# A fused attention and expert layer on one core: the router as ranks in 14 steps, and a new order of the steady batch

## The chip, the cores and the metric

The kernel runs on one core of a Trainium2 chip. The metric is the device time of one execution in microseconds (us); less is better.

## What is computed

The input x is 4 batches of 1024 rows of 128 channels. With `ln` for a layer norm without weights:

```
x = x + ln(attn(ln(x)));   attn(y) = y + ripple(y)
x = x + ln(ffn(ln(x)))
ripple: q, k, v = y @ Wqkv, 8 heads of 16
        every row looks at the rows 0, 1, 2, 4, ... 512 above it (11 terms), softmax over them
        + a causal convolution of v with 7 taps for each channel
        + linear attention (elu(q)+1, elu(k)+1) over the whole batch;  then @ Wo
ffn:    scores = sigmoid(y @ gate_W) * route_scale; the best 2 of 8 experts, their scores
        divided by their sum; sum over them of gate * (gelu(y @ W1[e] + b1) @ W2[e] + b2)
        + gelu(y @ Ws1 + bs1) @ Ws2 + bs2
```

## The kernel before, in words

Five engines run programs written out by hand: PE (matmuls, and transposes as matmuls with an identity), DVE, ACT, POOL and SP (which issues loads, stores and copies). Semaphores connect them; each engine takes its instructions in the written order. So the order of the calls in each engine's loop `for b in range(B + 1)` is the schedule, and nothing else plans it.

A batch is handled in two layers that overlap. In the round b the engines do the attention of batch b, and beside it the expert layer of the two halves of batch b-1: the units u0 = 2b-2 and u1 = 2b-1 of 512 rows each. The fifth round (b = 4) has only the expert layer of the last batch. Rounds 1 and 2 are the steady ones; round 3 has no next batch to prepare.

The steps of a round, by the names of the code:

- DVE: `residual(2b-2)` closes the first half of the former batch and opens the round. Then the key and query features (`key_features`, `query_features`), three groups of `products` (q times a shifted k, L284), `stats` of the batch after (L904), `linear_state` (its `kv` is L961), `residual(u1)`, the router `gates(u0)` (L1105 to L1155), `softmax_logits`, `gate_hidden(u0)` (L1164), `softmax_weights`, and eight tiles of `weigh` (L1021), which make the 11 weighted terms of each row, with the steps of `gates(u1)` among them. `add_conv` (L1041) adds the convolution to a finished half.
- PE: `sum_heads` (L1366) sums the products, `turn_scores`, `low`, `gates_expert_major` turns the gates, `hidden` (L1460) and `experts_out` (L1500, a tile of 128 rows with five matmuls) are the expert layer; `turn_x3`, `gate_logits` and `turn_logits` begin a unit; `sum_terms` (L1395, L1398) adds the terms of a tile; `turn_x`, `project_k`, `project_q`, `project_v` make the next batch's keys, queries and values. `keep_busy` (L1509) turns the identity, with no result that anything reads.
- ACT: copies PSUM to SBUF (L573), scales the convolution's taps (`scale_taps`, L640), normalises (`normalise1`, L584, for the next batch; `normalise3`, L698, for a unit of the expert layer), takes the squares of the norms (`norm2`, `norm3_squares`, `norm4`), and all of Exp and Gelu. Exp and Gelu are in different tables, and each change of table is an ACT_TABLE_LOAD.
- POOL: `ln1` to `ln4` raise variances to the power -1/2, and `sum_taps_first`, `_second` and `_third` issue copies between tiles in SBUF that add one scaled tap to another.
- SP: loads of x, 19 copies per batch that shift v by 1 to 64 rows (`shift_v`), stores.

The router of a unit (`gates`) works on a tile of 128x32 (four tiles of rows, 8 experts). Before the change it has 24 steps, one DVE instruction each, that wait for one another: sigmoid (0 to 2), the largest score and the first expert that has it (3 to 7), the same for the second (8 to 13), weights (14 to 18), and the gates as a sum of three bf16 parts (19 to 23). Steps 0 to 3 of u0 stand between the third products and `kv`; the others behind `residual(u1)`. The 24 steps of u1 are spread over the tiles 1 to 4 of `weigh`, six for each.

A few waits matter below. `scores` on ACT needs `sum_heads(b, 2)`, which needs `kv`. The tile j of `weigh` needs `sum_terms(j-4)`. `add_conv(b, 0)` needs `sum_terms(3)` and the sum of all taps. `residual(2b)` needs `ln2`, that needs `norm2(2b)`, that needs `output(b, 0)`; on ACT, `norm2(2b)` stands behind `key_parts` and `query_parts` of the next batch.

## Time and profile before

| | us |
|---|---|
| three runs | 281.3, 281.8, 281.28 |
| median | 281.3 |
| the profiled execution | 281.24 |
| its span, first to last instruction | 279.5 |
| PE busy | 252.3 (90%) |
| DVE busy | 234.2 (84%) |
| ACT busy | 188.7 (68%) |
| POOL busy | 88.0 (31%) |

The span is the time between the first and the last instruction of the profiled execution; 1.74 us of its time lie around it. PE is busy with `keep_busy` too, so its share says less than it seems. The chain of waits that ended last is made of PE by 56%, ACT by 20%, DVE by 14%, POOL by 4%. The granted TensorE clock is 0.99 of full speed in the mean.

### The profile page before, as it was taken

Reading aid. Unit: us, or ns where it says so; the run is one execution under the profiler, and the core shown is the slowest. Engines: PE = TensorE matmul, PEld = TensorE weight load, DVE = VectorE, ACT = ScalarE, POOL = GpSimd, SP = SyncE. Lnnn points to the kernel's source line nnn. Section 1 sums busy time; section 2 is a strip of 40 time slices with the busy share of each in tenths; the row PEclk is TensorE's granted clock in tenths of the full one; section 3 lists DMA queues with packets and bytes.
Section 4 is the critical chain, followed back from the end, with each engine's and each line's share of the span. In section 5 each row is a group of like instructions: output and inputs, shape, how many; then the busy total and the mean of one; then the engine's idle time right before and its main releaser. Section 6 shows DMA issues by size and latency. Waiting matters only on the chain.

```text
span 279.5 us, 4820 instructions
## 1 busy us (share of the span) xinstructions
PE 252.3 (90%) x1640; PEld 175.4 (63%) x1640; DVE 234.2 (84%) x615; ACT 188.7 (68%) x444; POOL 88.0 (31%) x144
## 2 busy tenths in 40 slices
PE   5899999895988899998978899998989799999993
PEld 5444656885435686787635686787646677884483
DVE  7799899879988867999889967999599899858933
ACT  2482256638978766949798767959798546557831
POOL 5960300045471124044562114044232132431013
PEclk9999999997999999999999999999999999999998
DMA  7437801000799954401799972101799963000012
GB/s 194 100 98 242 236 19 59 1 0 5 218 230 196 233 113 83 121 1 38 245 234 208 211 137 43 49 5 32 244 217 228 230 122 73 17 0 1 0 40 75
DMA packets 23395, 32.12 MB, mean 115 GB/s; under 512 B 3958, under 2 KB 17103, under 8 KB 23371
## 3 DMA queue, kind: packets, MB, share of 16 engines
q1 hardware_dynamic: 20346, 21.59, 27.0%
q0 software_dynamic: 3024, 10.22, 20.1%
q8 instruction: 13, 0.21, 0.3%
q14 instruction: 12, 0.09, 0.1%
HBM read 5.07 MB, written 2.10 MB: 26 GB/s over the span
## 4 chain that ended last, share of the span: by engine, by line
PE 56%; ACT 20%; DVE 14%; POOL 4%; issue 3%; DMA 1%; POOLq 0%; DVEq 0%; ACTq 0%
PE psH L1398 11%; PE psF L1460 7%; PE psY L1500 6%; PE psG L1320 4%; PE psA L1366 4%; PE psA L1292 4%; DVE prods L284 3%; PE psA L1500 3%; POOL rstd L468 2%; ACT squares L691 2%; ACT xn L584 2%; ACT xn L698 2%; PE psG L1486 2%; DVE prods L1021 2%; PE psH L1395 2%
## 5 line engine op out<-in xcount | busy, mean ns | idle before, releaser
L284 DVE TENSOR_TENSOR prods<-qT,kT 128x1024 f32<-128x1024 f32 (+1 forms) x48 | 50.7, 1111 | 2.7 <-PE psA L1366 1.6
L466 POOL TENSOR_SCALAR var<-ss 128x4 f32<-128x4 f32 (+1 forms) x24 | 8.3, 345 | 102.0 <-ACT squares L684 46.3
L1398 PE MATMUL psH<-ident,prods 128*128 128x128 f32 x324 | 40.0, 273 | 0.0
L468 POOL TENSOR_TENSOR rstd<-var,neg_half 128x4 f32<-128x4 f32 (+2 forms) x27 | 38.1, 1412 | 2.2
L1398 PEld LDWEIGHTS psH<-ident,prods 128*128 128x128 f32 x324 | 36.4, 141 | 2.9 <-issue 2.9
L1021 DVE TENSOR_TENSOR prods<-v_shift,prob 128x896 f32<-128x896 f32 x32 | 34.6, 1082 | 0.0
L1460 PE MATMUL psF<-x3T,w 128*128 128x512 f32 x58 | 29.4, 614 | 1.4 <-ACT hid L722 1.4
L1366 PE MATMUL psA<-prods,slot_sel 128*32 128x512 f32 x168 | 23.0, 598 | 3.4 <-DVE kv L961 2.3
L722 ACT ACTIVATE hid<-psF,b1c 128x512 f32<-128x512 f32 x29 | 19.2, 690 | 6.6 <-PE psF L1460 6.5
L1164 DVE TENSOR_TENSOR hid<-hid,psG 128x512 f32<-128x512 f32 x30 | 19.3, 681 | 3.3 <-PE psG L1486 3.3
L1021 DVE TENSOR_TENSOR prods<-v_tok,prob 128x128 f32<-128x128 f32 (+2 forms) x60 | 20.8, 369 | 0.1
L1292 PE MATMUL psA<-xnT,wqkv 128*128 128x512 f32 x36 | 17.2, 601 | 1.5 <-ACT xnT L573 1.5
L1500 PEld LDWEIGHTS psY<-w,hid 128*128 128x128 f32 x140 | 16.6, 192 | 1.5 <-issue 1.4
L1500 PE MATMUL psY<-w,hid 128*128 128x128 f32 x140 | 17.6, 277 | 0.0
L1460 PEld LDWEIGHTS psF<-x3T,w 128*128 128x128 f32 x58 | 9.5, 189 | 11.1 <-issue 8.6
L1366 PEld LDWEIGHTS psA<-prods,slot_sel 128*32 128x32 f32 x168 | 5.4, 108 | 17.4 <-issue 8.3
L691 ACT ACTIVATE squares<-x,neg_mean 128x128 f32<-128x128 f32 x24 | 9.3, 391 | 8.7 <-DVE x L1052 8.7
L1320 PE MATMUL psG<-vT,tapT 128*128 128x512 f32 x28 | 12.8, 596 | 0.0
L1509 PE MATMUL psG<-ident 128*128 128x128 f32 x62 | 9.6, 321 | 3.1 <-POOL ident L419 3.1
L698 ACT ACTIVATE xn<-x,nmr,rstd 128x128 f32<-128x128 f32 x24 | 9.8, 482 | 3.7 <-POOL nmr L519 3.7
L1041 DVE TENSOR_TENSOR prods<-psH,convT 128x512 f32<-128x512 f32 x8 | 5.5, 692 | 8.1 <-PE psH L1398 7.9
L584 ACT ACTIVATE xn<-x_in,nmr,rstd 128x128 f32<-128x128 f32 x24 | 9.9, 487 | 3.2 <-POOL nmr L484 3.2
(247 smaller groups left out, 590.9 us busy)
## 6 DMA issues: line engine op xcount, KB each, us to landing
v_shift<-v_tok SPq DMA_DIRECT2D x20, 448.0 KB
convT<-tapT POOLq DMA_DIRECT2D x6, 512.0 KB, 6.0
x_res<-L_attn_x SPq DMA_DIRECT2D x4, 512.0 KB, 9.5
out<-y_out SPq DMA_DIRECT2D x7, 256.0 KB, 2.3
x_in<-L_attn_x SPq DMA_DIRECT2D x3, 512.0 KB, 4.0
v_shift<-v_tok SPq DMA_DIRECT2D x4, 384.0 KB
tapT<-tapT POOLq DMA_DIRECT2D x3, 512.0 KB, 11.5
convT<-kexp POOLq DMA_DIRECT2D x3, 512.0 KB, 9.1
```

What stands on the lines that cost most here:

```text
L284: return eng.tensor_tensor(prods[:, QUADS * (s % 2) + q, t0:t1], qT[:, t0:t1], kT[:, PRE - off + t0:PRE - off + t1], ALU.mult)
L468: return nc.gpsimd.tensor_tensor(rstd[:, cols], var[:, cols], neg_half[:, cols], ALU.pow)
L584: nc.scalar.activation(xn[:, j, :], x_in[:, j, :], ACT.Identity, bias=nmr1[:, j:j + 1], scale=rstd1[:, j:j + 1]).then_inc(xn_ready, 1)
L722: nc.scalar.activation(hid[:, c, half_cols(u)], hidden_bank(u, c), ACT.Gelu, bias=b1c[:, c:c + 1]).then_inc(hidden_free, 1)
L1021: return nc.vector.tensor_tensor(dst, src.rearrange("p m (h d) -> p m h d", d=HD), w, ALU.mult)
L1164: nc.vector.tensor_tensor(hid[:, c, cols], hid[:, c, cols], spread_bank(u, c), ALU.mult).then_inc(gated, 1)
L1292: pe.matmul(psA[:, half, :], wqkv[:, bass.ts(part, P)], xnT[(b + 1) % 2][:, bass.ts(half, HALF)], start=True, stop=True).then_inc(psA_full, 1)
L1320: ins = pe.matmul(psG[:, half, :], tap_diag[:, TAPS - 1 - tap, :], vT[:, VPRE - tap + half * HALF:VPRE - tap + (half + 1) * HALF], start=( ...
L1366: ins = pe.matmul(psA[32 * q:32 * q + 32, half, :], ksum_sel[:] if low else slot_sel[:, s, :], fqT[:, cols] if low else prods[:, QUADS * ( ...
L1398: ins = pe.matmul(dst, terms[:, j % TERM_BUFS, m, :], ident[:], is_transpose=True, start=False, stop=(m == live[-1]))
L1460: pe.matmul(hidden_bank(u, c), w1[:, bass.ts(c, P)], x3T[:, half_cols(u)], start=True, stop=True).then_inc(hidden_full, 1)
L1500: ins = pe.matmul(output_tile(u, n), hid[:, c, bass.ts(j, P)], w2[:, c, :], start=(c == CH - 1), stop=(c == CH - 2))
```

## The change

It has five parts.

1. **Router.** `gates` has 14 steps. Steps 3 to 5 compare each score with each other one of its row (128x256 elements, in the tile `above`, which lies in `folded`), with a constant `tie_bar` that lets the lower expert win a tie, and count how many are above it. A rank under 1.5 is one of the best two. The tail takes four steps instead of five. The steps of u0 all stand behind `residual(u1)`; those of u1 stand in the tiles 2 to 4 of `weigh`, 4 + 6 + 4.
2. **ACT in a round.** `normalise1` of the next batch goes from around `scores` to behind the exponentials, among `normalise3(u1)`, `evacuate_x3` and `evacuate_shared`; `norm3_squares(u1)` goes behind `scores`; `evacuate_q` goes behind `scale_outputs(u0)`, the last step before `key_parts`; the values and keys by rows (`token_major_v`, `token_major_fk`) go ahead of the first tap; `norm4` of the former u1 goes behind the taps 2 and 3.
3. **PE in a round.** `turn_x` goes from ahead of the exponentials to behind `turn_logits(u1)`, `project_k` among the terms at j = 1 and `project_q` at j = 5, `output(b, 0)` from j = 4 to j = 6. The 18 turns of `keep_busy` become 8 and 8; the 14 ahead of `output(b, 1)` become a tile of `experts_out(u1)`.
4. **POOL in a round.** `ln1(b+1)` goes from ahead of the first tap sum to behind `ln3(u1)`, ahead of the second.
5. **The last rounds.** In round 3 two tiles of `experts_out(u1)` stand around the last `sum_terms`; the first unit of the last batch is normalised by DVE, the second by ACT (before: the other way about); in round 4 `keep_busy` goes, `experts_out(u0-1)` is split around `gate_logits`, and `gate_hidden` follows the steps 6, 9, 14 and 14 of `gates(u1)`.

The diff, cut to its core:

```diff
@@ gates @@
-                    elif n == 3:
-                        ins = red(m1, score, AX_X, ALU.max)
-                    elif n == 4:
-                        ins = tt(eq, score, spread(m1), ALU.is_equal)
...
+                    elif n == 3:
+                        ins = tt(above, score.unsqueeze(2).to_broadcast(pair), score.unsqueeze(3).to_broadcast(pair),
+                                 ALU.subtract)
+                    elif n == 4:
+                        ins = tt(above, above, tie_bar[:].unsqueeze(1).to_broadcast(pair), ALU.is_gt)
+                    elif n == 5:
+                        ins = red(rank, above, AX_X, ALU.add)
+                    elif n == 6:
+                        ins = nc.vector.scalar_tensor_tensor(out=both, in0=rank, scalar=1.5, in1=score,
+                                                             op0=ALU.is_lt, op1=ALU.mult)
...
@@ DVE, round @@
-                    products(b, 2, range(0, 1))
-                    products(b, 2, range(1, 3), gate_step_of(u0, 0))
-                    linear_state(b, gate_step_of(u0, 2))
+                    products(b, 2)
+                    linear_state(b)
...
-                        gates(u0, range(4, 24))
+                        gates(u0, range(N_GATE_STEPS))
...
@@ POOL, round @@
-                    if more:
-                        ln1(b + 1)
                     if b >= 2:
                         ln4(u0 - 1)
-                    if b:
+                    if b == 0:
+                        ln1(b + 1)
+                    else:
                         sum_taps_first(b)
                         ln3(u1)
+                        if more:
+                            ln1(b + 1)
                         sum_taps_second(b)
...
@@ PE, round @@
-                        if more and j == 1:
+                        if more and ffn and j == 1:
+                            project_k(b + 1)
+                        if more and j == (5 if ffn else 1):
                             project_q(b + 1)
                         sum_terms(b, j)
-                        if j == TPH:
+                        if j == (6 if ffn else TPH):
                             output(b, 0)
+                        if not more and j >= 6:
+                            experts_out(u1, (j - 6,))
...
@@ the round's last lines on DVE @@
                     else:
-                        gate_hidden(u1, range(2, 4))
+                        last_normalise()
```

**ACT, third round, around the exponentials** (L672, L680 after: the exponentials; L584, L592: `normalise1`; L691, L699: `norm3_squares`; `prods<-psA`: `scores`). Before:

```order
L584 ACTIVATE xn<-x_in,nmr,rstd 128x128 x4
L691 ACTIVATE squares,ss<-x,neg_mean 128x128 x4
L573 ACTIVATE prods<-psA 128x512 x2
L584 ACTIVATE xn<-x_in,nmr,rstd 128x128 x4
L722 ACT_TABLE_LOAD
L722 ACTIVATE hid<-psF,b1c 128x512 x2
L573 ACTIVATE gT<-psG 24x512
L573 ACTIVATE hid<-gT 24x512
L722 ACTIVATE hid<-psF,b1c 128x512 x2
L726 ACTIVATE hid<-gate_shared,bs1c 64x512
L672 ACT_TABLE_LOAD
L672 ACTIVATE prob<-prob 128x768
```

After the change:

```order
L581 ACTIVATE prods<-psA 128x512 x2
L699 ACTIVATE squares,ss<-x,neg_mean 128x128 x4
L730 ACT_TABLE_LOAD
L730 ACTIVATE hid<-psF,b1c 128x512 x2
L581 ACTIVATE gT<-psG 24x512
L730 ACTIVATE hid<-psF,b1c 128x512 x2
L581 ACTIVATE hid<-gT 24x512
L734 ACTIVATE hid<-gate_shared,bs1c 64x512
L680 ACT_TABLE_LOAD
L680 ACTIVATE prob<-prob 128x768
L706 ACTIVATE xn<-x,nmr,rstd 128x128 x4
L592 ACTIVATE xn<-x_in,nmr,rstd 128x128 x4
```

Both halves of `normalise1` have left the stretch from the scores to the exponentials and stand behind them.

**ACT, third round, its end** (L722, L730: Gelu of `hidden`; squares of psY: `norm4(u0)`; L755, L763: `scale_outputs`; L647, L655: the first part of `key_parts`). Before:

```order
L722 ACT_TABLE_LOAD
L722 ACTIVATE hid<-psF,b1c 128x512 x2
L746 ACTIVATE squares,ss<-psY 128x128 x4
L573 ACTIVATE qT<-psA 128x512 x2
L755 ACTIVATE y_out<-psY,rstd 128x128 x4
L722 ACTIVATE hid<-psF,b1c 128x512 x2
L726 ACTIVATE hid<-gate_shared,bs1c 64x512
L573 ACTIVATE gT<-psG 24x512
L573 ACTIVATE hid<-gT 24x512
L647 ACT_TABLE_LOAD
L647 ACTIVATE kexp<-kT 128x1024
```

After:

```order
L730 ACT_TABLE_LOAD
L730 ACTIVATE hid<-psF,b1c 128x512 x2
L581 ACTIVATE kT<-psA 128x512 x2
L730 ACTIVATE hid<-psF,b1c 128x512 x2
L754 ACTIVATE squares,ss<-psY 128x128 x4
L734 ACTIVATE hid<-gate_shared,bs1c 64x512
L581 ACTIVATE gT<-psG 24x512
L581 ACTIVATE hid<-gT 24x512
L763 ACTIVATE y_out<-psY,rstd 128x128 x4
L581 ACTIVATE qT<-psA 128x512 x2
L655 ACT_TABLE_LOAD
L655 ACTIVATE kexp<-kT 128x1024
```

The copies of the queries (`qT`) stood ahead of `scale_outputs` and two Gelu; now they are the last work before the table load.

**PE, third round, among the terms** (L1500, L1478: `experts_out`; L1460, L1438: `hidden`; L1292, L1270: a projection; L1395 with L1398, L1373 with L1376: `sum_terms`). Before:

```order
L1292 MATMUL psA<-xnT,wqkv 128x512 x2
L1395 MATMUL psH<-ident,prods 128x128
L1398 MATMUL psH<-ident,prods 128x128 x9
L1460 MATMUL psF<-x3T,w 128x512 x2
L1395 MATMUL psH<-ident,prods 128x128
L1398 MATMUL psH<-ident,prods 128x128 x10
L1395 MATMUL psH<-ident,prods 128x128
L1398 MATMUL psH<-ident,prods 128x128 x10
L1470 MATMUL psG<-identb,gparts 24x128 x4
L1395 MATMUL psH<-ident,prods 128x128
L1398 MATMUL psH<-ident,prods 128x128 x11
L1408 MATMUL psY<-wo,prods 128x128
```

After:

```order
L1478 MATMUL psY<-w,hid 128x128 x5
L1373 MATMUL psH<-ident,prods 128x128
L1376 MATMUL psH<-ident,prods 128x128 x10
L1438 MATMUL psF<-x3T,w 128x512 x2
L1373 MATMUL psH<-ident,prods 128x128
L1376 MATMUL psH<-ident,prods 128x128 x10
L1448 MATMUL psG<-identb,gparts 24x128 x4
L1373 MATMUL psH<-ident,prods 128x128
L1376 MATMUL psH<-ident,prods 128x128 x11
L1464 MATMUL psG<-gT,gate_sel 128x512 x2
L1270 MATMUL psA<-xnT,wqkv 128x512 x2
L1373 MATMUL psH<-ident,prods 128x128
```

The first rows are the projection (queries) before, and after it the last tile of `experts_out(u0)`; the queries now follow the fifth tile of terms.

## Rows read from the trace of the kernel before

**Rows 1.** Busy time by stage: stretch, length, PE, PEld, DVE, ACT, POOL, clock, DMA
```profile
59.23:121.24 62.01, 55.24 (x362) 38.08 (x360) 53.75 (x139) 49.56 (x110) 21.50 (x23) 0.97 0.59 135
121.24:184.22 62.98, 58.45 (x402) 41.34 (x400) 54.65 (x144) 50.45 (x118) 21.90 (x25) 1.00 0.55 129
184.22:247.11 62.89, 57.70 (x416) 42.57 (x414) 54.58 (x140) 45.23 (x121) 20.63 (x26) 1.00 0.56 130
247.11:279.50 32.39, 27.20 (x162) 18.34 (x162) 19.92 (x79) 16.29 (x45) 5.19 (x9) 0.96 0.08 25
```

**Rows 2.** Waits of DVE: us in total, times, longest us
```profile
DVE gtmp L1105 <- ACT gexp L714: 9.4, 6, 2.4
```

**Rows 3.** Timeline, DVE, third batch: start us, us, line, operation
```profile
140.46 0.28 DVE L961 TENSOR_TENSOR kv<-psY,head_mask 128x128 f32<-128x128 f32 x1
143.81 0.18 DVE L1113 TENSOR_TENSOR gtmp<-gtmp,gmax 128x32 f32<-128x32 f32 x1
148.02 0.18 DVE L1155 CAST gparts<-gtmp 128x32 bf16<-128x32 f32 x1
```

**Rows 4.** Groups by shape, DVE: count, busy us, mean ns, idle before
```profile
L967 DVE TENSOR_TENSOR folded<-prob 128x384 f32<-128x384 f32 x8 | 4.4, 555 | 0.8 <-ACT prob L672 0.6
L1021 DVE TENSOR_TENSOR prods<-v_tok,prob 128x256 f32<-128x256 f32 x8 | 3.3, 417 | 0.0
L919 DVE TENSOR_REDUCE row_mean<-w 128x5 f32<-128x640 f32 x1 | 0.8, 812 | 0.0
```

**Rows 5.** Timeline, PE, third batch
```profile
140.89 0.63 PE L1366 MATMUL psA<-prods,slot_sel 128*32 128x512 f32 x3 [0.89 <-DVE kv L961]
145.38 1.14 PE L1284 MATMUL psA<-ident,prods 128*128 128x128 f32 x8 [0.65 <-ACT prods L573]
152.01 1.04 PE L1284 MATMUL psA<-ident,xn 128*128 128x128 f32 x8
158.44 0.63 PE L1430 MATMUL psF<-ident,xn 128*128 128x128 f32 x4
174.49 0.39 PE L1470 MATMUL psG<-identb,gparts 128*24 128x128 bf16 x4
175.44 0.30 PE L1395 MATMUL psH<-ident,prods 128*128 128x128 f32 x1 [0.55 <-DVE prods L1041]
```

**Rows 6.** Timeline, ACT, third batch, middle
```profile
152.21 0.69 ACT L722 ACTIVATE hid<-psF,b1c 128x512 f32<-128x512 f32 x1 [0.59 <-PE psF L1460]
156.66 1.64 ACT L698 ACTIVATE xn<-x,nmr,rstd 128x128 f32<-128x128 f32 x4
```

**Rows 7.** Timeline, ACT, POOL and DVE, end of the third batch
```profile
176.19 1.28 ACT L647 ACT_TABLE_LOAD   x1
177.48 1.06 ACT L647 ACTIVATE kexp<-kT 128x1024 f32<-128x1024 f32 x1
182.78 1.03 POOL L468 TENSOR_TENSOR rstd<-var,neg_half 128x4 f32<-128x4 f32 x1
184.22 1.11 DVE L1052 SCALAR_TENSOR_TENSOR x<-psY,rstd,x_res 128x128 f32<-128x128 f32 x4
```

**Rows 8.** Timeline of PE after two gaps, and the busy times at the first
```profile
66.03 1.97 PE L1284 MATMUL psA<-ident,vT 128*128 128x128 f32 x8 [2.87 <-ACT vT L573]
218.89 0.63 PE L1430 MATMUL psF<-ident,xn 128*128 128x128 f32 x4 [1.84 <-ACT xn L698]
66.00:67.00 1.00, 0.96 (x5) 0.97 (x6) 1.00 (x2) 0.97 (x2) 0.90 (x1) 0.50 0.00 0
```

**Rows 9.** Timeline, POOL, second and fourth batch
```profile
75.80 2.57 POOL L468 TENSOR_TENSOR rstd<-var,neg_half 128x8 f32<-128x8 f32 x1
227.09 0.86 POOL L487 DMA_DIRECT2D convT<-tapT  x1 [7.21 <-DMA convT<-fkT]
```

**Rows 10.** Timeline, DVE, last part
```profile
251.44 0.18 DVE L1105 TENSOR_SCALAR gtmp<-gexp 128x32 f32<-128x32 f32 x1 [1.49 <-ACT gexp L714]
256.75 0.18 DVE L1155 CAST gparts<-gtmp 128x32 bf16<-128x32 f32 x1
```

265 lines of the change are left out of this document (115 added, 150 removed).

## The prediction

> **What bounds the kernel now.** I read the busy times by stage first. I cut the span where DVE starts `residual(2b)`, since the whole round hangs on it, and the last part where PE starts the front of the last batch [rows 1]. The rounds 1, 2 and 3 take 62.01, 62.98 and 62.89 us, the last part 32.39. In round 2 PE is busy for 58.45, DVE for 54.65, ACT for 50.45: all three are dense, none is the bound alone. So the shares don't price an edit; the chain through a round does. The waits say where DVE, which does the router, stands still: 9.4 us in six waits for the exponentials of the router's logits [rows 2]. I then followed round 2 through the timelines and give its times from its start (121.24 us = 0).
>
> In round 2 the chain is this. DVE starts `kv` at 19.2 [rows 3]; PE sums the scores from 19.65, and turns them from 24.1, held by ACT, whose `norm3_squares` and first half of `normalise1` stand ahead of the copy of the scores [rows 5]. The last Gelu of u0 starts at 31.0, `normalise3(u1)` at 35.4 [rows 6], `turn_x3(u1)` on PE at 37.2, the turn of the gates behind the fourth tile of terms at 53.25 [rows 5]. From there DVE has its last four tiles, and ACT ends with a table load at 54.95 and the key and query parts; POOL's `ln2` lets DVE start the next round at 62.98 [rows 7].
>
> **The router.** A chained step on 128x32 costs DVE 0.22 us: 19 of them from 143.81 to 148.02 [rows 3]. Steps 0 to 2 stay. Steps 3 and 4 are now 128x256: 0.42 us is the row for that many elements, 0.56 that for 384 [rows 4]; I take 0.45 with the chain's gap. For the reduction of 256 elements the row has 640 in 0.81 us [rows 4]; 0.42 lies between that over 2.5 (0.33) and 0.5. For u0: 0.86 (steps 0 to 2), 0.45 + 0.45 + 0.42, and eight steps of 0.22, is 3.9 us, where 0.75 + 4.4 stood before: 1.2 less. For u1 the hidden gaps make it 1.0 less. Of these 2.2 us per round only what lies ahead of the scores can reach the chain, below. With both bounds of the new steps (3.7 and 4.5 us) u0's gates end at 23.8 to 24.6, and PE wants them at 24.5, so this price hardly matters in the steady rounds.
>
> **The front of a round.** Steps 0 to 3 of u0 (0.75 us) and their wait (one of the six of [rows 2], about 1 us) leave the stretch ahead of `kv`: it starts at 17.6, not 19.2. PE starts the last sums of scores at 18.0. ACT has only the copies of the scores to do, and PE's 0.65 us of waiting for them [rows 5] goes. Its queue (sums 1.86, two `hidden` 1.75, the turn 0.97, `low` 1.9, from differences of starts) ends at 24.5. Then the turn of the gates, two `hidden`: the last Gelu of u0 starts at 26.7, 4.3 us sooner. From that Gelu to `normalise3(u1)` ACT took 4.45 us [rows 6]; without the copies of `turn_x` (0.96) and with the gates' row (0.6) it takes 4.1: 30.8. PE follows 1.78 later, at 32.5 instead of 37.2. What hides the moved `normalise1`: in the old place it was in this chain, 3 us of ACT; in the new one half of it delays the x3 copy by 0.3.
>
> **The middle.** From `turn_x3(u1)` to the turn of u1's gates PE took 16.05 us, without a gap worth naming [rows 5]. The same work now has `turn_x` in it, 0.97 (152.01 to 152.98 [rows 5]); `project_k` stands where `project_q` stood. With 0.4 us of waits for ACT's two copies this is 17.3: 49.8, 3.4 us sooner. DVE is at 45.4 by then and waits.
>
> **The end of a round.** Here the time goes again. `add_conv(b, 0)` and the restart of the terms take 0.95 us (174.49 to 175.44 [rows 5]), the tile 1.3, two spreads 0.5, `project_q` 1.7: PE has the queries at 54.3. ACT has been full since 48.7 (last Gelu, `norm4`, shared Gelu, gates, `scale_outputs`, which waits for POOL). It ends the copy of the queries at 55.1. From the table load to DVE's start of the next round it took 8.03 us [rows 7], of which DVE was late by 0.3, since `ln2` ended at 183.81 [rows 7]: 7.7. The round is 62.8 us long. So round 1 gets 0.8 us longer and round 2 0.2 shorter: DVE's and PE's head start of 4 us ends in a wait for `norm2(2b)`, which stands behind the key and query parts. Their table load starts at 55.1, no sooner than the 54.95 of before [rows 7], since the work between `turn_x3(u1)` and it has grown from 17.8 to 22.6 us.
>
> What else is moved: the 18 + 14 turns of `keep_busy` cost nothing as work, and neither does their going. `ln1(b+1)` on POOL took some 5 us in round 1, its power alone 2.57 [rows 9], and now stands ahead of the second tap sum. That starts at 28.7 instead of 28.6, for the first one starts 2.3 us sooner; the queue of four sums ends at 47 or 48 and is wanted at 49.9. SP's 19 copies of v start 2.1 us sooner, because `token_major_v` is ahead of the first tap; their terms are wanted 2.7 sooner, with some 5 us to spare in round 2. The load of the next x waits for `normalise1`, 10 us later than before, but stands in SP's queue behind a store that is later still. All of these at nothing.
>
> **Round 3 and the last part.** Without `stats` the front gains another 0.9 us: `turn_x3(u1)` at 31.3. PE has no projection in the middle: the fourth tile is done at 45.7. But the sum of taps ends there: its last addition was issued at 42.9 after 7.2 us of waiting [rows 9], and the terms that follow may wait half a us for it. Behind it `output(b, 0)` now comes after the seventh tile, at 54 instead of 51.3, then `norm2`, `ln2`, `residual`, `last_normalise`: I get 0.6 us less than the 62.89 [rows 1]. In the last part the gates of u0 took 5.4 us [rows 10], now 4.0; but PE's queue and ACT's four Gelu wait for the second table load, 0.8 us later. Walked through, the last experts end 0.5 us sooner.
>
> **TensorE's clock.** PE stood idle for 2.87 us at the start of round 1, and behind that the clock is 0.50 of full, its 1.2 GHz level; eight turns took 1.97 us, where 1.14 is usual [rows 5, 8]. Behind a gap of 1.84 us in round 3 it was full [rows 8]. In the new order PE ends its last `keep_busy` ahead of `turn_x3(u1)` at 29.5 in round 1, 30.2 in round 2 and 29.3 in round 3, so the gaps are 3.0, 2.3 and 2.0 us. I take a fall in round 1 alone. The old fall cost 1.2 us of PE's work; here a part lies under waits for ACT: 0.8. The bounds are 0 and 1.3 for each of three rounds. The Trainium skill, "TensorE: Matmul & The Clock Gate", Part 4: PE-mode transpose, says that a transpose doesn't count as PE busy. By that rule `keep_busy`, which is nothing but transposes, would hold no clock, and the clock would fall in all three rounds. The trace speaks against it: 24 transposes and the gap of 1.84 us left the clock full.
>
> **The sum.** Round 1 +0.8, round 2 -0.2, round 3 -0.6, last part -0.5, clock +0.8: +0.3 us on the profiled execution's 281.24, which is 0.06 below the median. I forecast 281.5 us: no change that 0.2% (0.56 us, about what a measurement of this kernel can tell) would show.
>
> The Trainium skill, "ScalarE: Activation LUTs", What ACT_TABLE_LOAD costs, has 2.66 us for a change of table. In the trace it is 1.29, from 176.19 to 177.48 [rows 7], and I use that. By the page's figure the two changes on the new chain would make the round an estimated 65.5 us.
>
> **Rivals.**
> - *The order fits better than I walk it* (faster). The small waits that I put in (0.4 for the copies, 0.95 at `add_conv`, 0.5 at the taps) go under one another, and the clock stays up. For it: PE ran its 16.05 us without such waits [rows 5], and an error in the middle counts in three rounds. Against it: each wait has a row like it. Without the fall, and with 1 us less in each round, it is 281.24 - 0.5 - 3.1, about 277.6 us. Chance 0.3.
> - *The clock falls in all three rounds* (slower). The point is a gap between 1.84 and 2.87 us; the gaps of 2.3 and 2.0 lie between. Three falls at 1.2 us each on the 280.7 without one give 284.3; it decides in `turn_x3(u1)`, which the chain passes. Against it: the fall behind 2.87 us began only after 2 us of idling, and the two shorter gaps end about there. Chance 0.25.
> - *The change doesn't do what it says*: the ranks give the same gates with 10 instructions fewer, and the orders above show that the moves are made. I give this no chance.
>
> Chances: forecast 0.45 (of which 0.12 under 280.7 and 0.13 over 281.9), fast rival 0.3, slow rival 0.25. Faster by over 0.2% is 0.12 + 0.28 = 0.40, same 0.22, slower 0.13 + 0.25 = 0.38. The range reaches from near the fast rival to near the slow one: 277.8 to 284.2. The forecast's own case is 280.3 to 282.7.
>
> **What would show it.** Right: `turn_x3(u1)` 32 to 33 us behind the start of rounds 1 and 2, the turn of u1's gates at 49 to 50.5, ACT without a gap from the last Gelu to `norm2(2b)`, DVE waiting about 1.5 us for POOL ahead of `residual(2b)`, rounds of 62.3 to 63.3. The first gates of a unit take 3.7 to 4.5 us. A granted clock of 0.5 in round 1 around 32 us. Wrong: rounds under 61.5 us with ACT waiting at their end, or a wait of `add_conv` for a DMA, or 0.5 behind `turn_x3(u1)` in all rounds.

## The result, and the profile after

The changed kernel takes 290.25 us in the median of four runs (288.8 to 290.31), before takes 281.34 (281.28 to 281.8). The ratio is 1.030, with a 95% interval of 1.028 to 1.032: slower by 8.9 us. I had forecast 281.5 us and a range up to 284.2. The ratios in this document leave disturbed executions out, as the comparisons do.

| | before | after |
|---|---|---|
| profiled execution | 281.24 us | 290.23 us |
| its span | 279.5 us | 288.4 us |
| PE busy | 252.3 us (90%) | 252.3 us (87%) |
| DVE busy | 234.2 us (84%) | 227.8 us (79%) |
| ACT busy | 188.7 us (68%) | 189.2 us (66%) |
| mean granted clock | 0.990 | 0.966 |

The stages first, cut as in [rows 1]: rounds 1, 2 and 3 and the last part (stretch, length, then the busy time of PE, its weight loads, DVE, ACT and POOL, the granted clock, DMA).

```profile
59.15:125.35 66.20, 58.74 (x375) 39.86 (x373) 52.15 (x119) 49.87 (x110) 19.58 (x23) 0.95 0.55 127
125.35:190.55 65.20, 58.11 (x385) 40.72 (x384) 53.18 (x123) 50.86 (x118) 22.43 (x25) 0.97 0.54 125
190.55:255.50 64.95, 56.06 (x377) 40.54 (x377) 53.26 (x117) 43.63 (x117) 19.57 (x26) 0.95 0.54 125
255.50:288.40 32.90, 26.43 (x152) 17.48 (x152) 17.82 (x64) 17.61 (x50) 6.38 (x11) 0.96 0.08 25
```

Against [rows 1] that is +4.19, +2.22, +2.06 and +0.51 us. The time doesn't come from more work: in all, DVE is busy for 6.4 us less, PE for as long as before, ACT for 0.5 us more. What changed with the length of the rounds is the clock: 0.95, 0.97, 0.95, where it was 0.97, 1.00 and 1.00.

Where does it fall? PE's timeline at the last sums of scores in round 1, and at `turn_x3(u1)` and the turn of the logits behind it in all three rounds:

```profile
77.19 0.73 PE L1344 MATMUL psA<-prods,slot_sel 128*32 128x512 f32 x3 [3.12 <-DVE kv L968]
...
79.34 1.14 PE L1344 MATMUL psA<-prods,slot_sel 128*32 128x512 f32 x3
...
93.39 0.63 PE L1408 MATMUL psF<-ident,xn 128*128 128x128 f32 x4 [2.70 <-ACT xn L706]
...
98.85 0.41 PE L1420 MATMUL psF<-ident,gate_shared 8*128 8x8 f32 x4
...
143.40 0.63 PE L1344 MATMUL psA<-prods,slot_sel 128*32 128x512 f32 x3 [0.96 <-DVE kv L968]
...
158.69 0.63 PE L1408 MATMUL psF<-ident,xn 128*128 128x128 f32 x4 [2.05 <-ACT xn L706]
...
164.00 0.41 PE L1420 MATMUL psF<-ident,gate_shared 8*128 8x8 f32 x4
...
222.07 1.09 PE L1408 MATMUL psF<-ident,xn 128*128 128x128 f32 x4 [2.04 <-ACT xn L706]
...
228.47 0.41 PE L1420 MATMUL psF<-ident,gate_shared 8*128 8x8 f32 x4
```

And the granted clock, over one us at the last sums of round 1 and behind each of the three `turn_x3(u1)` (stretch, length, PE busy, clock, DMA):

```profile
78.00:79.00 1.00, 1.00 (x8) 0.50 0.93 242
95.00:96.00 1.00, 1.00 (x4) 0.50 0.89 180
160.00:161.00 1.00, 1.00 (x7) 0.50 1.04 206
222.00:223.00 1.00, 0.93 (x5) 0.50 0.89 194
```

At 0.50 PE runs on its 1.2 GHz level, at 1.00 on 2.4. Read the fence ahead of it by durations: a sum of three at 77.19 takes 0.73 us, one at 79.34 takes 1.14, the usual (143.40) is 0.63. The last sums of round 1 take 3.23 us (77.19 to 80.42), where those of round 2 take 1.85. From `turn_x3(u1)` to the end of the turn of the logits (start to start of the work behind it) it is 5.80, 5.65 and 6.75 us, and 3.99 us in round 2 of before (158.44 [rows 5] to 162.43). With the clock held it is 4.50, 4.51 and 3.99 in the new order, as the first experiment shows; in rounds 1 and 2 PE waits 0.28 us of it for ACT's copy of x3. So PE lost 1.4 us at the sums, and 1.3, 1.15 and 2.75 behind `turn_x3`. In that order the clock stays low for 3.4, 3.4, 3.4 and 6.8 us. I had forecast one fall, in round 1, for 0.8. The old fall at the start of round 1, behind the gap of 2.87 us [rows 8], is gone: PE turns the values at 63.08 without a wait.

Now the steps that I had named, in round 2 (125.35 us = 0), in the timelines: `kv`, the wait of `finish`, and the router's first step on DVE, the two turns of the gates on PE, and at the end ACT's table load, POOL's `ln2` and DVE's next round:

```profile
142.96 0.29 DVE L968 TENSOR_TENSOR kv<-psY,head_mask 128x128 f32<-128x128 f32 x1
144.09 1.13 DVE L1159 SCALAR_TENSOR_TENSOR y_out<-psG,rstd,x 128x128 f32<-128x128 f32 x4 [0.84 <-POOL rstd L471]
...
146.40 0.17 DVE L1108 TENSOR_SCALAR gtmp<-gexp 128x32 f32<-128x32 f32 x1
...
150.57 0.38 PE L1448 MATMUL psG<-identb,gparts 128*24 128x128 bf16 x4 [0.68 <-DVE gparts L1140]
...
177.23 0.39 PE L1448 MATMUL psG<-identb,gparts 128*24 128x128 bf16 x4
...
182.82 1.28 ACT L655 ACT_TABLE_LOAD   x1
...
189.42 1.03 POOL L471 TENSOR_TENSOR rstd<-var,neg_half 128x4 f32<-128x4 f32 x1
...
190.55 1.12 DVE L1058 SCALAR_TENSOR_TENSOR x<-psY,rstd,x_res 128x128 f32<-128x128 f32 x4 [1.75 <-POOL rstd L471]
```

`kv` starts at 17.6, as forecast. The gates' turn comes at 25.2 (forecast 24.5), `turn_x3(u1)` at 33.3 (32.5), the turn of u1's gates at 51.9 (49.8), the table load at 57.5 (55.1), the next round at 65.2 (62.8). The router is as forecast too: u0's first step at 146.40, its last ends at 150.43, 4.0 us (forecast 3.9).

### The profile page after: what moved, and what is told of

Read it like the earlier page. It is cut to its first block, busy times and chain, and to the rows that moved or that the text cites. A ratio compares the mean times of both kernels' runs of the same rounds, so it can differ in the third digit from the quotient of the medians.

```text
span 288.4 us, 4645 instructions
## 1 busy us (share of the span) xinstructions
PE 252.3 (87%) x1590; PEld 173.1 (60%) x1590; DVE 227.8 (79%) x535; ACT 189.2 (66%) x445; POOL 86.9 (30%) x139
## 4 chain that ended last, share of the span: by engine, by line
PE 57%; ACT 19%; DVE 13%; POOL 6%; issue 3%; POOLq 0%; DVEq 0%; ACTq 0%
PE psF L1438 9%; PE psH L1376 7%; PE psY L1478 7%; PE psA L1344 6%; POOL rstd L471 4%; PE psG L1298 4%; DVE prods L286 4%; PE psF L1415 3%; PE psA L1262 3%; ACT xn L706 3%; PE psA L1270 2%; PE psA L1478 2%; ACT squares L699 2%; POOL var L469 2%; PE psF L1408 1%
## 5 line engine op out<-in xcount | busy, mean ns | idle before, releaser
L469 POOL TENSOR_SCALAR var<-ss 128x4 f32<-128x4 f32 (+1 forms) x24 | 11.3, 471 | 127.9 <-ACT squares L754 66.8
L1376 PE MATMUL psH<-ident,prods 128*128 128x128 f32 x324 | 40.2, 273 | 0.0
L1376 PEld LDWEIGHTS psH<-ident,prods 128*128 128x128 f32 x324 | 36.4, 141 | 3.4 <-issue 3.4
L471 POOL TENSOR_TENSOR rstd<-var,neg_half 128x4 f32<-128x4 f32 (+2 forms) x27 | 37.0, 1370 | 2.2
L730 ACT ACTIVATE hid<-psF,b1c 128x512 f32<-128x512 f32 x29 | 19.4, 683 | 15.5 <-PE psF L1438 15.1
L1438 PE MATMUL psF<-x3T,w 128*128 128x512 f32 x58 | 28.7, 613 | 0.3 <-ACT gexp L722 0.3
L1344 PE MATMUL psA<-prods,slot_sel 128*32 128x512 f32 x168 | 24.2, 624 | 4.1 <-DVE kv L968 4.1
L1478 PEld LDWEIGHTS psY<-w,hid 128*128 128x128 f32 x140 | 20.2, 222 | 3.1 <-issue 3.1
L1478 PE MATMUL psY<-w,hid 128*128 128x128 f32 x140 | 21.0, 306 | 0.0
L1270 PE MATMUL psA<-xnT,wqkv 128*128 128x512 f32 x36 | 17.2, 601 | 0.3 <-ACT xnT L581 0.3
L1438 PEld LDWEIGHTS psF<-x3T,w 128*128 128x128 f32 x58 | 10.0, 194 | 11.1 <-issue 10.3
L699 ACT ACTIVATE squares<-x,neg_mean 128x128 f32<-128x128 f32 x24 | 9.3, 395 | 7.6 <-DVE x L1058 7.6
L1408 PE MATMUL psF<-ident,xn 128*128 128x128 f32 x28 | 4.9, 302 | 10.6 <-ACT xn L706 9.0
L1373 PE MATMUL psH<-ident,prods 128*128 128x128 f32 x32 | 9.1, 283 | 3.4 <-DVE prods L1047 2.5
L490 POOL DMA_DIRECT2D convT<-tapT x6 | 5.5, 919 | 20.6 <-DMA convT<-fkT 14.5
```

The source lines that it names most:

```text
L469: nc.gpsimd.tensor_scalar(var[:, cols], src, scale, EPS, ALU.mult, ALU.add).then_inc(step, 1)
L471: return nc.gpsimd.tensor_tensor(rstd[:, cols], var[:, cols], neg_half[:, cols], ALU.pow)
L730: nc.scalar.activation(hid[:, c, half_cols(u)], hidden_bank(u, c), ACT.Gelu, bias=b1c[:, c:c + 1]).then_inc(hidden_free, 1)
L1270: pe.matmul(psA[:, half, :], wqkv[:, bass.ts(part, P)], xnT[(b + 1) % 2][:, bass.ts(half, HALF)], start=True, stop=True).then_inc(psA_full, 1)
L1344: ins = pe.matmul(psA[32 * q:32 * q + 32, half, :], ksum_sel[:] if low else slot_sel[:, s, :], fqT[:, cols] if low else prods[:, QUADS * ( ...
L1376: ins = pe.matmul(dst, terms[:, j % TERM_BUFS, m, :], ident[:], is_transpose=True, start=False, stop=(m == live[-1]))
```

## The experiments

The theories: **the clock** (gaps on PE, which the new order makes and its fewer `keep_busy` turns don't fill, bring the clock down in each round, and PE is in the chain there), and against it **the new chain** (without any fall the new order is longer by itself, above all at the end of a round). A third: the router, or the sum of the taps, is what holds.

### More turns ahead of `turn_x3(u1)`

```diff
-FILL_LOW, FILL_LAST, FILL_K, FILL_OUT = 8, 8, 8, 14
+FILL_LOW, FILL_LAST, FILL_K, FILL_OUT = 8, 24, 24, 14
```

> The changed kernel with 24 turns instead of 8 in the last fill ahead of turn_x3(u1), in rounds 1 to 3. From turn_x3(u1) to the end of the turn of the logits PE took 5.80, 5.65 and 6.75 us in the three rounds of the changed kernel, where the same work took 4.06 in round 2 of before. Theory 1 (most of the loss is the clock, and idling of PE ahead of turn_x3(u1) brings it down): the gaps of 2.70, 2.05 and 2.04 us shrink to about 0.9, 0.3 and 0.3, the clock stays at its upper level behind them, the three stretches take 4.1 us each, and 6.0 us go: 284.2 us, bounds 283.2 and 285.5. Theory 2 (the new chain is longer by itself, and the clock is beside the chain): under 2 us go, 288.3 or more. Theory 3 (turns do not count as work for the clock, whatever their number): the clock falls as before and the time stays at 290.2.

Measured: 285.54 us in the median of four (284.57 to 288.49), ratio to before 1.014 (1.008 to 1.021). The work added makes the kernel 4.7 us faster. PE in round 1, at the last sums and at `turn_x3(u1)`, and at the start of round 2, where the clock still fell:

```profile
77.44 0.63 PE L1344 MATMUL psA<-prods,slot_sel 128*32 128x512 f32 x3 [3.12 <-DVE kv L968]
...
92.00 0.63 PE L1408 MATMUL psF<-ident,xn 128*128 128x128 f32 x4 [0.96 <-ACT xn L706]
...
96.16 0.41 PE L1420 MATMUL psF<-ident,gate_shared 8*128 8x8 f32 x4
...
126.25 1.52 PE L1262 MATMUL psA<-ident,vT 128*128 128x128 f32 x8 [1.86 <-ACT vT L581]
```

The median lies at the upper bound (285.5) that I had set for theory 1. The stretch from `turn_x3(u1)` (92.00) to the next work (96.50) is 4.50 us, in rounds 2 and 3 it is 4.51 (156.00 to 160.51) and 3.99 (219.16 to 223.15), and the clock is full behind all three gaps. What the kernel got instead are falls in another place, at `token_major_v` at the start of rounds 2 and 3: eight turns in 1.52 us behind a gap of 1.86. The changed kernel has a gap of 1.85 us in the same place, at 128.94, with the clock at 1.00 behind it. At the last sums the gap is 3.12 us, to the hundredth that of the changed kernel (77.19 above), and the clock stays up: a sum takes 0.63 us. Theory 1 holds, at 4.7 us and not 6.0. A part of the difference is that I had reckoned with 4.06 us for each of the three stretches, and two take 4.5. Another is round 3: its stretch is 2.75 us shorter than in the changed kernel, the round only 1.23 (63.72 us), and DVE waits 2.00 us for the tap sum at `add_conv(b, 0)` now. The new falls cost little where they are: round 2 of this execution is 64.05 us long with one, and 64.06 in the kernel with both fills below without one. Its round 1 is 63.26 us, 2.94 shorter than in the changed kernel, and 1.4 of that is the fall at the sums, which the edit didn't touch. Theory 3 of the list, that turns don't count, falls.

### Products instead of turns

```diff
-                    pe.transpose(bank[:, bass.ts(k % TPH, P)], ident[:], ident[:])
+                    pe.matmul(bank[:, bass.ts(k % TPH, P)], ident[:], ident[:], start=True, stop=True)
```

> The changed kernel with all fills as plain products of the identity with itself instead of transposes of it, the same number in the same places, so that all gaps stay as long as they are. Theory 1a (the length of the gap alone decides): the clock falls in the same places, 290.2 us. Theory 1b (transposes do not count for the clock, as the Trainium skill, TensorE: Matmul & The Clock Gate, Part 4: PE-mode transpose, has it, and products do): behind the gaps of 2.05 and 2.04 us in rounds 2 and 3 the clock stays up, and 4.3 us go: 286.0 us; behind the 2.70 us of round 1 it may fall still.

Measured: 286.69 us (285.75 to 290.5, four runs), ratio 1.015 (1.011 to 1.020). It tells less than I wanted: a product of fp32 runs as two instructions and takes twice as long as a turn, so the gaps of 2.05 us shrank to 0.79, and the gap, not the kind of work, may be what changed. The profiled run is the one of 290.5 us, with a start 3 us longer and a fall in the last part. But its three rounds are all at a full clock, so they show what the new order costs by itself (the kernel with both fills, below, has the same lengths in an execution of 285.99 us):

```profile
62.67:125.92 63.25, 59.04 (x405) 41.97 (x404) 51.98 (x120) 49.64 (x110) 19.03 (x23) 1.00 0.57 133
125.92:189.92 64.00, 58.36 (x401) 41.62 (x400) 53.08 (x123) 50.75 (x118) 22.39 (x25) 1.00 0.55 127
189.92:253.11 63.19, 54.99 (x393) 40.27 (x393) 53.30 (x117) 43.48 (x117) 18.24 (x26) 1.00 0.56 129
```

63.25, 64.00 and 63.19 us against 62.01, 62.98 and 62.89 [rows 1]: +1.2, +1.0, +0.3. To part kind and length I ran this, with fewer products:

```diff
-FILL_LOW, FILL_LAST, FILL_K, FILL_OUT = 8, 8, 8, 14
+FILL_LOW, FILL_LAST, FILL_K, FILL_OUT = 3, 3, 3, 14
...
-                        keep_busy(FILL_LOW, front(u1, X3))
+                        products_instead(FILL_LOW, front(u1, X3))
```

> The changed kernel, its two fills of 8 transposes of the identity ahead of turn_x3(u1) replaced by 3 products of it with itself each (a product of fp32 took two instructions and 0.27 us in the kernel with all fills as products, so 6 take about 1.6 us, where the 16 turns take 1.8), so that the gaps ahead of turn_x3(u1) are 2.2 us or longer in all rounds, no shorter than in the changed kernel. If the length of the gap decides: falls as in the changed kernel, mean clock 0.966, 290 us. If a transpose does not count as work for the clock and a product does: the clock stays up in rounds 2 and 3 at least, mean clock 0.98 or more, 286 us.

Measured: 288.68 us (288.25 to 290.57), ratio 1.027 (1.020 to 1.035), mean clock 0.97. The clock falls in all three rounds. The last fill and `turn_x3(u1)` in round 3:

```profile
217.30 0.94 PE L1486 MATMUL psF<-ident 128*128 128x128 f32 x6
220.43 1.09 PE L1408 MATMUL psF<-ident,xn 128*128 128x128 f32 x4 [2.20 <-ACT xn L706]
```

The clock over one us in round 2:

```profile
154.00:155.00 1.00, 1.00 (x6) 0.50 0.94 203
```

Products, and a gap of 2.2 us, and the turns of `turn_x3` still take 1.09 us instead of 0.63. The gap isn't the same everywhere: in round 1 it is 2.87 us, in round 2 only 1.75, and there the fall comes 1.1 us ahead of the gap, while PE is fully busy. The Trainium skill, "TensorE: Matmul & The Clock Gate", Part 4: PE-mode transpose, says that a transpose doesn't count as PE busy the way other work does. Neither run bears that out for the fp32 turns of this kernel: 24 turns in the last fill held the clock at `turn_x3(u1)`, and 3 products in place of each 8 turns, about as long, didn't. Per round, fills of 3.9 us of turns and of 4.1 us of products (all fills as products) held it; 2.2 us of turns and 1.9 us of products didn't.

### No fill at all

```diff
-FILL_LOW, FILL_LAST, FILL_K, FILL_OUT = 8, 8, 8, 14
+FILL_LOW, FILL_LAST, FILL_K, FILL_OUT = 0, 0, 0, 14
```

> The changed kernel without the two fills of 8 turns ahead of turn_x3(u1), rounds 1 to 3: the gaps grow by 1.8 us to 4.5, 3.9 and 3.8 us. If turns count as work, the clock falls 1.8 us sooner and the granted clock is low over more of the gap and less or as much of the work behind it: 289 to 291 us. If turns do not count at all, nothing changes in any row behind the gap: from turn_x3(u1) to the end of the turn of the logits 5.8, 5.65 and 6.75 us as before, 290.2 us.

Measured: 290.01 us (289.01 to 290.18), ratio 1.029 (1.023 to 1.035), mean clock 0.964. The fall starts sooner. In round 2 it begins at 155.5, behind a wait of 1.33 us for the spread gates and 0.4 us ahead of the gap of 2.95 (the clock over one us in the gap, and where the fall ends):

```profile
156.00:157.00 1.00, 0.00 (x0) 0.50 1.11 313
162.00:163.00 1.00, 1.00 (x4) 0.81 0.49 98
```

The clock is low for 6.8 us from 155.5 on, in the changed kernel for 3.4 us from 159.5 on; the sooner and longer fall lies for a good part in the gap, and the round is as long (65.22 us against 65.20). So 16 turns of fill bought nothing (290.0 against 290.25), and 32 bought 4.7 us. A fill that is too short was no better than none here.

### A fill ahead of the last sums as well

```diff
+                    if b == 1:
+                        pe.wait_ge(front_free, upto(u0, N_FRONT, 2))
+                        keep_busy(FILL_SUMS, hidden_bank(u0, 0))
                     sum_heads(b, 2)
```

with `FILL_SUMS = 24`, on top of the 24 turns ahead of `turn_x3(u1)`.

> As the kernel with 24 turns ahead of turn_x3(u1), and 24 turns more ahead of the last sums of scores in round 1, where PE idles for 3.12 us until kv is there, and the sums then took 3.23 us instead of the 1.86 of round 2. Theory 1: the clock stays up there too, and 1.6 us more go than with the fill at turn_x3(u1) alone: 282.6 us. Theory 2: nothing more than that kernel.

Measured: 284.18 us in ten runs (283.49 to 285.99), ratio 1.009 (1.006 to 1.012). By stage:

```profile
60.86:124.11 63.25, 60.03 (x415) 42.79 (x413) 51.98 (x119) 49.76 (x110) 19.51 (x23) 1.00 0.58 133
124.11:188.17 64.06, 58.43 (x401) 41.41 (x400) 53.13 (x123) 50.76 (x118) 22.43 (x25) 1.00 0.54 127
188.17:251.37 63.20, 56.52 (x393) 41.63 (x393) 53.27 (x117) 43.73 (x117) 18.48 (x26) 0.97 0.56 129
251.37:284.30 32.93, 26.43 (x152) 17.49 (x152) 17.84 (x64) 17.62 (x50) 6.38 (x11) 0.96 0.08 25
```

Rounds 1 and 2 are clean, 63.25 and 64.06 us. Against the changed kernel that is -2.95, -1.14 and -1.75: the fills give back 5.8 of the 8.9 us, and 6.1 by the medians. The further gain on the fill at `turn_x3(u1)` alone is 1.4 us by the medians, but it can't be put on the sums: in the profiled run of that kernel the clock had not fallen there, with the gap of 3 us in place. It hadn't in the profiled runs with few products and with no fill either, with gaps of 3.13 us. The fall at the sums is in one profile, that of the changed kernel.

Round 3 has a fall at its start here too, from 193.1 to 196.5, and is as long as the clean one above (63.20 and 63.19): a fall there costs nothing.

### The router alone, in the old order

```diff
-N_GATE_STEPS = 24
+N_GATE_STEPS = 14
...
-                        gates(u0, range(4, 24))
+                        gates(u0, range(4, N_GATE_STEPS))
```

and the body of `gates` as changed.

> The kernel before with the router of 14 steps alone, in the old order (four steps beside the products, ten behind residual(u1); u1's in pairs among the terms). Theory A (in the old order the router is beside the chain, which goes through ACT's norm, copies and Gelu): 281.3 us, within 0.3. Theory B (DVE is in the chain between residual(u1) and the exponentials): 1.0 us less DVE time in each of rounds 1 to 3 and 1.3 in the last part: 277.5 to 280.

Measured: 282.55 us in ten runs (281.04 to 284.17), beside 281.48 for before in 19 runs (281.19 to 282.95); ratio 1.002 (0.999 to 1.004). The medians are 1.1 us apart, more than the 0.3 that I had allowed theory A, but the executions of both kernels spread over more than that, and theory B's 277.5 to 280 is ruled out. Its `normalise3(u1)` starts on ACT at 156.83, where before has 156.66 [rows 6]: the DVE time saved doesn't reach the chain through ACT. Theory A fits.

### The first expert tile ahead of `turn_x3(u1)`

```diff
+                        experts_out(u0, (0,))
                         turn_x3(u1)
-                        experts_out(u0, (0,))
-                        gate_logits(u1)
                         experts_out(u0, (1,))
+                        gate_logits(u1)
+                        experts_out(u0, (2,))
```

`FILL_LAST` and `FILL_K` are 14 here, the rest as in the kernel with both fills.

> The kernel with 24 turns ahead of turn_x3(u1) and 24 ahead of round 1's last sums (284.2 us), and now the first tile of u0's expert outputs, 1.12 us of PE, ahead of turn_x3(u1) in place of 10 of the turns; the other tiles move one place forward. Theory (behind turn_x3(u1) PE is the chain, in a stretch of 32 us without gaps): 1.1 us less in each of rounds 1 to 3, 280.9 us, provided DVE's last product with the spread gates is done by then. Rival (ACT, not PE, sets the end of the round): at most 0.3 us a round, 283.3 us.

Measured: 283.65 us in ten runs, from 280.98 to 288.25; ratio 1.003 (0.999 to 1.007). The best runs are the 280.9 that I had worked out, the median isn't. In the profiled run rounds 1 and 2 take 62.1 and 62.9 us, 1.1 less each than with both fills, as the theory has it. That run has 287.02 us, and in round 3 a low clock in dense work:

```profile
233.00:234.00 1.00, 1.00 (x5) 0.50 0.00 0
240.00:241.00 1.00, 1.00 (x7) 0.50 0.00 0
```

PE had waited 1.91 us for `add_conv(b, 0)` up to 231.47; from 232.3 to 242.5 it is busy without a gap, and the clock is 0.50 all the time, 10.2 us. The falls of the changed kernel last 3.4 or 6.8 us. I have no cause for one of 10.

### The queries earlier

```diff
                             if j == 2:
-                                experts_out(u0, (3,))
-                            if j == 3:
                                 hidden(u1, range(2, 4))
+                            if j == 3:
+                                experts_out(u0, (3,))
...
-                        if more and j == (5 if ffn else 1):
+                        if more and j == (4 if ffn else 1):
```

and on ACT `evacuate_q(b + 1)` ahead of `scale_outputs(u0)`, in the kernel with both fills.

> The kernel with 24 turns ahead of turn_x3(u1) and 24 ahead of round 1's last sums (284.2 us), with the end of the round changed: hidden(u1) chunks 2 and 3 one tile earlier (ACT idled 3.67 us for them), project_q ahead of the fifth tile of terms instead of the sixth (PE idled 0.55 us there for add_conv), and ACT's copy of the queries ahead of scale_outputs, which waited 0.82 us for POOL. Theory (the end of a round goes through project_q, the copy of the queries and ACT's key and query parts, and that is where the head start of the front was lost): 1.5 us less in each of rounds 1 and 2, 281.2 us. Rival (the end hangs on output(b, 0) behind the seventh tile, not on the queries): within 0.5 us of 284.2.

Measured: 280.89 us in ten runs (280.12 to 281.64), ratio to before 0.997 (0.994 to 1.000). In round 2 (121.18 us = 0), on PE the turn of u1's gates and the queries, on ACT their copy and the table load, and DVE's next round:

```profile
171.87 0.39 PE L1450 MATMUL psG<-identb,gparts 128*24 128x128 bf16 x4
172.19 1.98 PE L1272 MATMUL psA<-xnT,wqkv 128*128 128x512 f32 x4
...
173.84 1.05 ACT L582 ACTIVATE qT<-psA 128x512 f32<-128x512 f32 x2
...
175.90 1.28 ACT L656 ACT_TABLE_LOAD   x1
...
183.62 1.13 DVE L1060 SCALAR_TENSOR_TENSOR x<-psY,rstd,x_res 128x128 f32<-128x128 f32 x4 [0.78 <-POOL rstd L472]
```

From the turn of the gates to the next round it is 11.75 us, where the changed kernel has 13.3. The wait at `add_conv` lies under the queries now, and ACT has no gap in that stretch. The expected 1.5 us in each of rounds 1 and 2 are there: rounds of 61.7, 62.4 and 62.2 us against 63.25, 64.06 and 63.2. This edit on the changed kernel, with its fills of 8 and none ahead of the sums:

> The changed kernel with the earlier queries alone, and its fills as they were (8, 8, none ahead of the sums). If the clock's loss and the end of the round are separate terms: the falls stay, mean clock 0.966, and 3.3 us go from 290.2: 286.9 us. If an earlier round hides the slow stretches, or the falls take the gain back: further off than 1 us.

Measured: 285.49 us (284.88 to 287.05), ratio 1.013 (1.009 to 1.017), mean clock 0.979: 4.8 us less than the changed kernel, not 3.3. The two terms aren't separate. In the profiled run the rounds take 62.9, 62.45 and 63.5 us: round 2 is as short as with the held clock (62.44), since it has no fall any more, and the fall at the sums of round 1 is gone too, with its gap of 3.12 us in place. Against that, the last part takes 34.1 us, with a fall from 250.9 on. The same gap of 2.04 us is there ahead of `turn_x3(u1)` in rounds 2 and 3, and the clock falls only at the second (four turns in 0.63 us, and in 1.09; that fall begins at 216.8, 0.6 us ahead of the gap's end):

```profile
156.72 0.63 PE L1409 MATMUL psF<-ident,xn 128*128 128x128 f32 x4 [2.04 <-ACT xn L706]
...
217.40 1.09 PE L1409 MATMUL psF<-ident,xn 128*128 128x128 f32 x4 [2.04 <-ACT xn L706]
```

### Both orders together, and what held them

The two diffs above in one kernel, with `FILL_LAST` and `FILL_K` 14 and `FILL_SUMS` 24:

> The two orders together: the first expert tile ahead of turn_x3(u1) with 14 turns in the last fill, and the earlier queries at the end of a round, with 24 turns ahead of round 1's last sums. If PE's 1.1 us per round and ACT's 1.6 us at the end of rounds 1 and 2 add up: 3.0 us under the 280.9 of the kernel with the earlier queries alone, 278 us, faster than before (281.35). If both shorten the same chain: 280 to 281. The kernel with the expert tile first had runs from 281 to 288 us with clocks of 1.0 to 0.964, so its best runs are what to compare, and the clock may fall here as well.

Measured: 12 runs from 277.19 to 286.3 us, median 282.17; ratio 0.988 (0.985 to 0.991), which rests on the four that took 277.2 to 279.4 us. The profiled execution isn't one of them, it took 282.22 us. Its rounds 1 and 2 take 60.6 and 61.1 us, so the tile ahead of `turn_x3(u1)`, with 10 turns fewer, is worth 1.1 and 1.35 us a round beside the kernel with the earlier queries, and the gains add up. Its round 3 takes 65.3. DVE waits 3.17 us there for the last addition of the tap sum, and a fall of the clock follows, from 230.3 to 233.7. The wait isn't new: with the clock held in the old tile order it was 2.00, 2.31 and 1.55 us in round 3 (24 turns, products, both fills). In round 3 of its timeline, the first addition of the tap sum on POOL, and DVE at `add_conv(b, 0)`:

```profile
199.09 0.93 POOL L491 DMA_DIRECT2D convT<-tapT  x1
...
229.97 0.69 DVE L1049 TENSOR_TENSOR prods<-psH,convT 128x512 f32<-128x512 f32 x1 [3.17 <-DMA convT<-tapT]
```

The same kernel with the router of 24 steps:

```diff
-N_GATE_STEPS = 14
+N_GATE_STEPS = 24
...
-                            first = 2 * (3 * (j - 2) + n - 1)
+                            first = 4 * (3 * (j - 2) + n - 1)
```

and the body of `gates` as before, with u1's steps four by four.

> As the kernel with both orders, but with the router of 24 steps: u0's gates take 5.15 us instead of 4.0, u1's steps go four by four beside the terms instead of two by two. If the router of ranks is beside the chain in the new order as it is in the old: within 0.5 us of the kernel with both. If PE's wait for u0's gates (0.6 us in round 2 before their turn) shows that DVE is in the chain there: 1.1 us in each of rounds 1 to 3 and 1.2 in the last part, 3 to 4.5 us slower.

Measured: 284.29 us in ten runs (282.89 to 290.88), ratio 1.006 (1.003 to 1.008). In the new order the router is in the chain, in rounds 2 and 3: PE waits 2.33 and 1.53 us for u0's gates, where the kernel with the ranks waits 0.39 and not at all; in round 1 neither waits. PE's waits by line (us in total, times, longest), and the wait of round 2:

```profile
PE psG L1467 <- DVE gparts L1159: 4.2, 3, 2.3
...
146.99 0.38 PE L1467 MATMUL psG<-identb,gparts 128*24 128x128 bf16 x4 [2.33 <-DVE gparts L1159]
```

The waits say 3.5 us. The medians of all runs are 2.1 us apart, but eight of the twelve with the ranks are over 281 us. The medians of those that the ratios rest on are 278.4 and 284.3, 5.9 apart, and the best runs 5.7. The 2 us beyond the waits can be the clock: behind the wait of 2.33 us it is low for 10.2 us, from 148.1 on. No run parts the two.

Last, the first two additions of the tap sum ahead of `ln4(u0-1)`:

```diff
-                    if b >= 2:
-                        ln4(u0 - 1)
                     if b == 0:
                         ln1(b + 1)
                     else:
                         sum_taps_first(b)
+                        if b >= 2:
+                            ln4(u0 - 1)
```

> As the kernel with both orders; on POOL the first two additions of the tap sum are issued ahead of ln4(u0-1) in rounds 2 and 3, not behind it. In round 3 of the kernel with both orders they were issued at 199.09, 2.6 us after the taps were scaled (196.6), the last of the four sums came late and DVE stood 3.17 us ahead of add_conv(b, 0) for it. Theory (the sum of taps through the DMA engines is what the new order runs into next): the additions go out 2.3 us or more sooner, the wait shrinks to 1 us or less, and the median falls from 282.2 to 279, with the best runs near 277. Rival (the DMA engines, 0.9 and more busy all through that stretch, set the end of the sums, not their start): the wait stays at 3 us, 282.

Measured: 278.33 us in ten runs (278.07 to 281.89), before 281.71 in the same comparison (281.17 to 283.13, 15 runs); ratio 0.990 (0.987 to 0.993). The same two rows of its timeline:

```profile
196.12 0.93 POOL L491 DMA_DIRECT2D convT<-tapT  x1 [7.07 <-ACT tapT L649]
...
227.30 0.69 DVE L1049 TENSOR_TENSOR prods<-psH,convT 128x512 f32<-128x512 f32 x1 [0.34 <-PE psH L1378]
```

And the three rounds:

```profile
59.40:120.01 60.61, 58.23 (x397) 40.88 (x395) 51.97 (x119) 49.56 (x110) 18.17 (x23) 1.00 0.59 138
120.01:181.37 61.36, 57.51 (x391) 40.41 (x390) 53.07 (x122) 50.58 (x118) 20.19 (x25) 1.00 0.58 133
181.37:243.52 62.15, 55.19 (x392) 40.07 (x391) 53.16 (x117) 43.62 (x117) 18.57 (x26) 1.00 0.57 131
```

The additions go out at 14.75 us of the round instead of 16.8 (2.05 sooner, a little less than I expected), and the wait for the DMA is gone. But the round 3 of 65.3 us is from an execution of 282.22 us, and the 62.15 from one of 278.15. The four best executions of the kernel without this edit have a median of 278.4 us and a ratio of 0.988: this one is no faster than they are. What differs is how many take over 281 us: 1 of 10, and 8 of 12 without the edit. Two sets of runs on two chips make that likely and don't show it. The edit has a price too: `ln4` comes later, and PE waits 0.68 us for u0's gates in round 2 (0.39 without it) and 1.10 in round 3 (none):

```profile
205.85 0.38 PE L1450 MATMUL psG<-identb,gparts 128*24 128x128 bf16 x4 [1.10 <-DVE gparts L1142]
```

This version beats both kernels: 1.0% less than before, 4% less than the changed kernel.

## Why the prediction was wrong

The miss is 8.75 us (290.25 against 281.5). The runs divide it so: the changed kernel has rounds of 66.2, 65.2 and 64.95 us; with the clock held (from the two kernels with clean rounds) they are 63.25, 64.05 and 63.2; I had 62.8, 62.8 and 62.3. So 5.9 us are the clock, of which I had 0.8 in the sum; 2.6 are the chain of the rounds; and 1.0 is the last part (32.9, I had 31.9).

- **The clock, +5.1. This is the step that failed:** "I take a fall in round 1 alone", at 0.8 us. There were two in round 1 and one in each of the others. I had looked at the gap ahead of `turn_x3(u1)` and read its length right (3.0, 2.3, 2.0 forecast; 2.70, 2.05, 2.04 measured). But I put a threshold between 1.84 and 2.87 us of gap, out of two cases. There is none in these runs: with 2.04 us the clock fell and did not fall in one execution, behind 1.86 it fell, with 3.12 it fell in the changed kernel and stayed in others. Its sign, 0.5 behind `turn_x3(u1)` in all rounds, was among those that I had named for being wrong. The slow rival (falls in all three rounds, chance 0.25) was the right mechanism. Its 284.3 was 6 us too low: 2.3 because it had 3.6 us for the clock, not 5.9 (no fall at the sums, and 1.2 us for each), and 3.6 in the rounds and the last part, which it took over from the forecast.
- **The gap that I left out.** I moved `kv` and found the sums of scores to start at 18.0 (right, 18.0). I didn't ask what PE would do until then. The work ahead of them ended sooner, because `token_major_v` and `token_major_fk` no longer wait behind the taps, and left 3.12 us idle in round 1: PE turns the values at 63.08 (66.03 [rows 8] before), and the last sums start at 77.19 (77.75 before). It is the same kind of view as the one I made at `turn_x3(u1)`, and I made it in one place only.
- **The price of a fall.** 1.2 us was the price of one that ran under eight turns. At `turn_x3(u1)`, where PE has dense work behind it, it is 1.15 to 2.75, and I had put the bound at 1.3. The 2.75 is the fall that lasts 6.8 us. At the start of rounds 2 and 3 of the kernels with the fills a fall of 3.4 us cost nothing in two rounds and half a us at most in a third.
- **The front, +0.85 in round 2** (the turn of the gates 0.7 late, `turn_x3(u1)` 33.35 against 32.5). u0's gates were right in length. But DVE began them late: `finish(u0-1)` waited 0.84 us for `ln4`, whose squares I had not followed on ACT behind taps 2 and 3. "This price hardly matters in the steady rounds" was wrong: PE waits 0.68 us for the gates, and 2.33 with 24 steps in the order of the last experiments.
- **The middle.** From `turn_x3(u1)` to the turn of u1's gates I had 17.3 us. With the clock held it is 17.4 (157.46 to 174.85 in the kernel with both fills); with the fall 18.5.
- **The end, +0.3.** From the turn to the next round I had 13.0, measured 13.3. That the head start would be lost there, behind ACT's queue, was right. It took one step more to see that the loss could be undone by the order of three calls.
- **Round 3, +0.9, and the last part, +1.0.** Round 3 has the same late gates and output as the others, and with the clock held PE waits 0.7 to 1.5 us at `add_conv(b, 0)`, behind the tap sum, where I had put half a us. In the last part I saw "the last experts end 0.5 us sooner"; it is 32.9 us against 32.39. One tile of u0's experts is done ahead of the last spreads, where before has two, so more of PE's work is left when the gates arrive. That is a reading of the order; I did no run on it, and the cause of the last part's 1.0 us stays open.
- **The tap sums at nothing:** right for this kernel, partly by luck. At `add_conv(b, 0)` in its round 3 DVE waits 2.72 us for PE, whose clock was low in that round. With the clock held ahead of it DVE waits 1.5 to 2.3 us for the DMA there.
- **The router, and `normalise1`:** the moves did what I said. The router by itself is worth nothing that these runs can tell in the old order.

## What to carry to other kernels

When an order is changed, list every gap of the engine with the granted clock, not only the one that the change is about: work that arrives sooner leaves the gap in front of what it waits for. Half a fill here was worth the same as none, and one that left 0.3 to 1.0 us of gap was enough. Ask of each fall what stands behind it: the same 3.4 us at half the clock cost 1.15 us or more in one place and nothing in another. And when the chain gets shorter, look for the transfer that used to be hidden with some slack: it can be the next bound. Before an edit is credited with a gain, look where each profiled execution lies among the times of its kernel.
